# A four-layer graph network on one core: block sums by register-addressed copies, stores in two pieces, scatters over 128 partitions

## The chip, the cores and the metric

The kernel runs on one core of one Trainium2 chip. The metric is the device time of one launch in microseconds (us). Before the change it is 10303.23 us, the median of three runs (10301.11 to 10311.45).

## The reference, cut to what matters

A graph of N = 12500 nodes with 64 features and E = 212500 edges, sorted by `dst`, goes through four layers, each on the normalised output of the one before:

```
for layer in (softmax aggregation, mean aggregation, hyperbolic attention, relational attention):
    h = maximum(layernorm(x), 0)
    x = x + layer(h, src, dst, ...)

# layer 2 (hyperbolic), cut to its end: hh, g are node tables made from h
ex          = exp(e - e_max[row])                      # one number for each edge
denom       = segment_sum(ex, row)                     # row = src, one sum for each node
att_log_h   = segment_sum(ex/denom[row] * log_h[col], row)
z           = elu(att_log_h) ... norm, tanh            # h_prime, added to x

# layer 3 (relational): 8 relations, 4 heads of 16
feat_all    = einsum('ni,rhid->rnhd', h, conv_weights) # per node: 8 x 64 features
el_all, er_all = feat_all . attn_l, feat_all . attn_r  # per node: 8 x 4 each
```

The edges of a layer are summed to nodes in one stage, and a "finish" stage turns the sums into the next layer's node tables.

## The kernel before, in words

Each stage is a `Block` in which every engine has its own hand-written program. A Block begins only when all engines have ended the one before, so the slowest engine, or the last DMA that one of them waits for, sets a stage's end. The order inside an engine is the order of the text. The stages are: the preparation of indices, `softmax_edges(0)`, `finish_softmax`, `mean_edges`, `finish_mean`, `hyperbolic_edges`, `finish_hyperbolic`, `softmax_edges(3)` and `finish_relational`. In the profiled execution `finish_mean` runs from 5685 to 6279 us, `hyperbolic_edges` up to 9477 us and `finish_hyperbolic` from there to 9904 us.

Node data lie on NP = 125 partitions with NB = 100 nodes each (node = p*100 + b). The constant `EVEN` is 112.

`hyperbolic_edges` writes running sums of 65 numbers (denominator and 64 message features) to the DRAM table `run_g`. For each of the BLOCKS = 98 blocks of 128 nodes, `final_g` holds the row of `run_g` from which that block's 128 final rows stand one after another.

`finish_hyperbolic` does the following.

- SyncE (SP) issues `load_indices` (eight loads of the edge indices `src3` into `idx_all`, used only in the next stage), then the load of `final_row`, eight loads of weights, `al` and `ar`. After that it stores one row group of `rows_o` to `table3s` for each of the 100 node groups g, into a ring of DEEP = 4 buffers.
- GpSimd (POOL) waits for `final_row`, gathers the sums of node column b from `run_g` into `acc[:, b, :]` in 100 indirect DMAs over 125 partitions (a quarter of them for each of the semaphores `got_acc[0..3]`), and only then scatters, for each group g, `dst_o[:, g]` to the rows `first_row` of `at_first`, once the group is taken (`lin3.taken`).
- VectorE (DVE) prepares the attention columns of `w_all`, and then for each quarter q of the nodes waits for `got_acc[q]`, computes the layer's output and the layernorm into `Hn`, and signals `h_ready`.
- TensorE (PE) transposes and multiplies one group at a time (`lin3.pe`, five matmuls).
- ScalarE (ACT) runs the roots and exponentials for DVE in between, copies the transposed rows (`lin3.act`) and takes the product into `rows_o` and `dst_o` (`take`). Before group 0 its text has `power(1)`, the exponential for quarter 1, which waits for DVE's `ask_exp` of that quarter. So PE's first product waits for the sums of the first 50 columns.

`finish_mean` is the stage in which the table of the hyperbolic layer is built: POOL gathers the last row of each node from the layer's scan (`gather_last`, 100 gathers over 128 partitions) and scatters the sorted runs (112 scatters). DVE waits for the first 20 gathers before its first product. The table is stored in two halves over 125 partitions at the end.

Of the kernel before, what the change touches and what calls it, by code (L numbers as in the profile page):

```python
# [75 lines left out]
def build(nc, x, src, dst, edge_attr, edge_type, w0a, b0a, gamma, beta, w0b, b0b, scale0,  # L76
          w1, b1, w2, c2, w3, al3, ar3, b3, out):
    with ExitStack() as whole:
# [10 lines left out]
        run_g = dram("run_g", ((NT + 1) * P, ACC2), F32)  # L89
        dst_i = dram("dst_i", (EP,), F32)  # L90
# [37 lines left out]
        first_row = sb("first_row", [NP, NB], I32)  # L128
# [255 lines left out]
        with nc.cleanup_on_exit(), ExitStack() as ctx:  # L384
# [19 lines left out]
            with nc.Block() as block:  # L404
# [37 lines left out]
                def _(dve):  # L442
# [3 lines left out]
                    dve.wait_ge(named, 1)  # L446
# [31 lines left out]
                    step(v.tensor_scalar(first_row[:, :], far_row[:, :], float(HALVES), None, ALU.mult))  # L478
# [1277 lines left out]
        def finish_mean():  # L1756

            with nc.cleanup_on_exit(), ExitStack() as ctx:
# [16 lines left out]
                        "n1_root n1_ask_tanh n1_tanhed n1_ask_log n1_logged n1_p n1_put n1_tabled n1_cready n1_croot n1_scattered", ctx)  # L1775
                nf, s1, tmp, th, np_, s2, k1, tn = (s[:, j, :] for j in range(4, 12))
# [163 lines left out]
        def finish_hyperbolic():  # L1940

            with nc.cleanup_on_exit(), ExitStack() as ctx:
                acc = sb("acc_s", [NP, NB, ACC2], F32, ctx)
                final_row = sb("final_row", [NP, NB], I32, ctx)
# [6 lines left out]
                dst_o = sb("dst_o", [NP, NB, RELS, HEADS], F32, ctx)  # L1951
                lin3 = Linear(ctx, "lin3", D, RELS * ROW3)
                got_acc = counter("n2_got_acc0 n2_got_acc1 n2_got_acc2 n2_got_acc3", ctx)
                got_w, ran, var_ready, std_ready, ask_root, root, ask_tanh, tanhed, ask_exp, exped, h_ready, got_final = counter(
                    "n2_got_w n2_ran n2_var_ready n2_std_ready n2_ask_root n2_root n2_ask_tanh n2_tanhed "
                    "n2_ask_exp n2_exped n2_h n2_got_final", ctx)
                put = counter("n2_put0 n2_put1 n2_put2 n2_put3", ctx)
                put_v, copied, got_idx = counter("n2_putv n2_copied n2_got_idx", ctx)
                EACH = NB // QUARTERS
                den, fac, tmp, zn, th, nf = (s[:, j, :] for j in range(4, 10))  # L1960
                with nc.Block() as block:
                    @block.sync
                    def _(sp):
                        load_indices(sp, src3, got_idx)
# [4 lines left out]
                        for t, a in ((al, al3), (ar, ar3)):  # L1969
                            sp.dma_start(t[:, :], spread_row(a.rearrange("r h d -> (r h d)"), D)).then_inc(got_w, 16)  # L1970
# [178 lines left out]
```

## Time and profile before

| | |
|---|---|
| timed runs | 10303.23 us median, 10301.11 to 10311.45 |
| profiled execution | span 12579.5 us; no other time is given for it, so its span stands for its own time |
| mean granted TensorE clock | 0.618 |
| busy share | PE 53%, DVE 56%, ACT 33%, POOL 59% |
| `finish_mean` | 5685 to 6279 us |
| `finish_hyperbolic` | 9477 to 9904 us |
| DMA queues | POOL's (software) 13.9% of 16 engines, SP's 11.4%, ACT's 8.9% |

The span of the profiled execution is 22% above the timed median. Times in rows are those of the profiled execution, from the start of its span. A row of a timeline has the start, the length, the engine, the line, the operation with its tiles, the count, and in brackets how long the engine was idle before it and what ended that.

### The profile page before, as it was taken

Reading aid. Unit: us, or ns where it says so; the run is one execution under the profiler, and the core shown is the slowest. Engines: PE = TensorE matmul, PEld = TensorE weight load, DVE = VectorE, ACT = ScalarE, POOL = GpSimd, SP = SyncE. Lnnn points to the kernel's source line nnn. Section 1 sums busy time; section 2 is a strip of 40 time slices with the busy share of each in tenths; the row PEclk is TensorE's granted clock in tenths of the full one; section 3 lists DMA queues with packets and bytes.
Section 4 is the critical chain, followed back from the end, with each engine's and each line's share of the span. In section 5 each row is a group of like instructions: output and inputs, shape, how many; then the busy total and the mean of one; then the engine's idle time right before and its main releaser. Section 6 shows DMA issues by size and latency. Waiting matters only on the chain. (4 is left out here: it accounts for less than half of the span.)

```text
span 12579.5 us, 120455 instructions
## 1 busy us (share of the span) xinstructions
PE 6684.8 (53%) x28159; PEld 5276.5 (42%) x28159; DVE 6985.0 (56%) x14192; ACT 4159.8 (33%) x8428; POOL 7375.6 (59%) x7574
## 2 busy tenths in 40 slices
PE   0555555543155555551356666666664655555552
PEld 0333333332145555550356666666662333333331
DVE  4555555565355555531645555555553377777775
ACT  0222222221055555550144444444442222222221
POOL 5666666652666666656055555555556566666665
PEclk9666666665577777775555555555555566666665
DMA  4333333332422222220033333333333344444442
GB/s 88 109 109 109 109 110 111 109 95 25 138 54 56 55 56 55 56 54 16 27 74 78 78 78 77 78 77 78 78 77 66 99 114 112 113 111 114 112 113 80
DMA packets 1318596, 1053.03 MB, mean 84 GB/s; under 512 B 817606, under 2 KB 1034525, under 8 KB 1317680
## 3 DMA queue, kind: packets, MB, share of 16 engines
q0 software_dynamic: 243008, 318.86, 13.9%
q1 hardware_dynamic: 677774, 367.08, 11.4%
q10 hardware_dynamic: 397397, 362.35, 8.9%
q8 instruction: 161, 2.64, 0.1%
q14 instruction: 256, 2.09, 0.1%
HBM read 577.78 MB, written 469.43 MB: 83 GB/s over the span
## 5 line engine op out<-in xcount | busy, mean ns | idle before, releaser
L1172 POOL DMA_INDIRECT h_rows_d<-table,h_idx_d x1840 | 1757.5, 955 | 1405.8 <-PE h_ps_sum L1193 831.4
L640 POOL DMA_INDIRECT rows<-table,idx_all x1664 | 1644.8, 988 | 879.3 <-issue 476.0
L947 POOL DMA_INDIRECT m_rows<-table,idx_all x1664 | 1574.9, 946 | 903.7 <-issue 452.1
L640 POOL DMA_INDIRECT rows<-table3s,idx_all x1664 | 1574.8, 946 | 893.0 <-issue 475.9
L977 PE MATMUL m_ps_sort<-m_hot_high,m_hot_low 128*128 128x224 f32 x3328 | 1050.7, 495 | 972.1 <-issue 817.5
L977 PEld LDWEIGHTS m_ps_sort<-m_hot_high,m_hot_low 128*128 128x128 f32 x3328 | 916.1, 281 | 1077.8 <-issue 938.9
L787 PE MATMUL ps_out<-ident,sums 128*128 128x128 f32 x3328 | 769.6, 397 | 986.9 <-issue 471.4
L1193 PE MATMUL h_ps_sum<-h_rows_d,h_hot 128*128 128x65 f32 x3680 | 829.3, 416 | 659.5 <-DVE h_rows_d L1330 364.9
L787 PEld LDWEIGHTS ps_out<-ident,sums 128*128 128x128 f32 x3328 | 630.3, 220 | 1149.2 <-issue 1041.8
L1193 PEld LDWEIGHTS h_ps_sum<-h_rows_d,h_hot 128*128 128x128 f32 x3680 | 792.7, 327 | 744.0 <-issue 744.0
L1211 PE MATMUL h_ps_src<-h_near,h_hot_t 128*128 128x65 f32 x3680 | 838.1, 419 | 457.9 <-DMA h_near<-table 266.9
L1211 PEld LDWEIGHTS h_ps_src<-h_near,h_hot_t 128*128 128x128 f32 x3680 | 803.2, 331 | 489.7 <-issue 489.0
L1040 DVE TENSOR_TENSOR_SCAN m_sums<-m_same_b,m_sums,m_ps_rows 128x512 f32<-128x512 bf16 x208 | 266.1, 1279 | 1075.2 <-issue 888.9
L827 ACT ACTIVATE out_e<-ps_out 128x512 f32<-128x512 f32 x832 | 445.8, 589 | 1119.2 <-remote 896.6
L1235 ACT ACTIVATE h_hot_t<-h_ps_hot 128x1024 f32<-128x1024 f32 x230 | 235.5, 1024 | 1580.4 <-DMA m_state_b<-scan 1487.7
L658 DVE TENSOR_TENSOR hot<-bins,cat 128x784 bf16<-128x784 bf16 x208 | 202.8, 975 | 945.3 <-DMA rows_p<-dst_i,row_i 848.7
L755 PE MATMUL ps_score<-ident,rows 128*128 128x128 f32 x1664 | 549.7, 425 | 282.4 <-issue 231.8
L1015 ACT ACTIVATE m_hot_low<-m_hot_low,record,m_slope 128x128 f32<-128x128 f32 x1664 | 660.1, 480 | 6.1
L1339 DVE SCALAR_TENSOR_TENSOR h_run<-h_run,h_goes_on,h_ps_sum 128x65 f32<-128x65 f32 x1840 | 518.9, 282 | 248.4 <-DMA final_g<-final_i 14.4
L1079 DVE SCALAR_TENSOR_TENSOR m_junk<-cat,m_ps_base 128x98 f32<-128x98 f32 (+61 forms) x1664 | 593.6, 419 | 91.1 <-issue 51.3
L667 DVE TENSOR_TENSOR_SCAN spread_v<-marks,spread_v,ps_v 64x512 f32<-64x512 bf16 x208 | 263.5, 1267 | 658.3 <-issue 640.0
L813 ACT ACTIVATE score_c<-ps_score 128x512 f32<-128x512 f32 x208 | 124.2, 597 | 1504.6 <-DMA table<-Hn 1219.9
(424 smaller groups left out, 14537.1 us busy)
## 6 DMA issues: line engine op xcount, KB each, us to landing
scan<-out_e ACTq DMA_DIRECT2D x832, 256.0 KB
h_near<-table SPq DMA_DIRECT2D x1840, 32.5 KB
run_g<-h_run ACTq DMA_DIRECT2D x230, 260.0 KB
part_b<-part SPq DMA_DIRECT2D x832, 64.0 KB
max_b<-top ACTq DMA_DIRECT2D x416, 128.0 KB
scan<-m_out_e SPq DMA_DIRECT2D x416, 128.0 KB
attr<-in_edge_attr SPq DMA_DIRECT2D x415, 128.0 KB
h_rows_d<-table,h_idx_d POOLq DMA_INDIRECT x1840
```

Source lines behind the costliest of these rows:

```text
L640: pool.indirect_dma_start(out=rows[:, b, k, h * GW:(h + 1) * GW], out_offset=None, in_=table3s.rearrange("n (q f) -> (n q) f", f=HEADS) if ...
L755: nc.tensor.matmul(ps_score[:, b % 2, k::TILES], rows[:, b, k, :], ident[:, :], start=True, stop=False)
L787: mm = nc.tensor.transpose(ps_out[:, j, k * P:(k + 1) * P], sums[:, b % 2, j, k::TILES], ident[:, :])
L827: ins = a.activation(out_e[:, b, :, :, j * D:(j + 1) * D], ps_out[:, j, :].rearrange("p (k h f) -> p h k f", k=TILES, h=HALVES), ACT.Copy)
L947: pool.indirect_dma_start(out=rows[:, b, k, h * D:(h + 1) * D], out_offset=None, in_=table1, in_offset=bass.IndirectOffsetOnAxis(ap=idx_al ...
L977: nc.tensor.matmul(ps_sort[:, 0:SORTED], hot_low[:, w % 2, j, :], hot_high[:, w % 2, j, :], start=n == 0, stop=n == PC - 1).then_inc(place ...
L1015: ins = a.activation(hot_low[:, w % 2, j, :], hot_low[:, w % 2, j, :], ACT.Relu, bias=record[:, at:at + 1], scale=slope[:, at:at + 1])
L1079: v.scalar_tensor_tensor(junk[:, at % 4, 0:BLOCKS + n], cat[:, p, 0:BLOCKS + n], cat[:, p, BLOCKS + n:BLOCKS + n + 1], ps_base[:, 0:BLOCKS ...
L1172: pool.indirect_dma_start(out=rows_d[:, b, k, :], out_offset=None, in_=table2, in_offset=bass.IndirectOffsetOnAxis(ap=idx_d[:, c * BT + k: ...
L1193: mm = nc.tensor.matmul(ps_sum[:, k // HB, (k % HB) * ACC2:(k % HB + 1) * ACC2], hot[:, b, k, :], rows_d[:, b, k, D + 1:ROW2], start=True, ...
L1211: mm = nc.tensor.matmul(ps_src[:, k // HB, (k % HB) * (D + 1):(k % HB + 1) * (D + 1)], hot_t[:, b % 2, k * P:(k + 1) * P], near[:, b, k, : ...
L1339: v.scalar_tensor_tensor(run[:, b, k, :], before, goes_on[:, bass.ds(c * BT + k, 1)], ps_sum[:, k // HB, (k % HB) * ACC2:(k % HB + 1) * AC ...
```

## The change

Four things change.

1. **Block sums.** A new DRAM tensor `acc_g` holds the final sums in node order. `finish_mean` loads the 98 first rows into `final_s` on one partition. In `finish_hyperbolic` SP and ACT each read 49 of these numbers into registers, seven at a time, and issue 49 copies from DRAM to DRAM of 128 rows each. When all 98 have landed, SP loads `acc` from `acc_g`, each quarter in two pieces. The 100 gathers and `final_row` are gone, so POOL has nothing before its scatters but a memset.
2. **Indices earlier.** `load_indices` for the last layer moves from `finish_hyperbolic` to SP's list in `finish_mean`.
3. **Stores in two pieces.** The two stores of the hyperbolic table in `finish_mean` and the 100 stores to `table3s` are split into partitions 0 to 111 and 112 to 124.
4. **Scatters over 128 partitions.** `first_row` and `dst_o` get 128 partitions; the three added ones scatter zeros to rows that nothing reads.

```diff
+        acc_g = dram("acc_g", (BLOCKS * P, ACC2), F32)
-        first_row = sb("first_row", [NP, NB], I32)
+        first_row = sb("first_row", [P, NB], I32)
+        final_s = sb("final_s", [1, BLOCKS], I32)
...
@@ preparation, POOL @@
+                    pool.iota(first_row[:, :], pattern=[[2, NB]], base=EP - 2 * N, channel_multiplier=2 * NB).then_inc(named, 1)
...
@@ finish_mean, SP @@
+                        sp.dma_start(final_s[:, :], final_g.rearrange("(b n) -> n b", n=P)[0:1, :],
+                                     allow_slow_non_contiguous=True).then_inc(got_final, 16)
+                        load_indices(sp, src3, got_idx)
                         for h, at in enumerate(halves):
                             sp.wait_ge(tabled, h + 1)
-                            sp.dma_start(nodes(table2[0:N, :])[:, at, :], table[:, at, :]).then_inc(put, 16)
-                        sp.wait_ge(put, 32)
+                            for some in (slice(0, EVEN), slice(EVEN, NP)):
+                                sp.dma_start(nodes(table2[0:N, :])[some, at, :], table[some, at, :]).then_inc(put, 16)
+                        sp.wait_ge(put, 64)
...
@@ finish_hyperbolic @@
+                FETCH = 7
+                def fetch_sums(eng, kind, lo, hi):
+                    for b0 in range(lo, hi, FETCH):
+                        _, rows = nc.values_load_multi_w_load_instructions(
+                            final_s[0:1, b0:b0 + FETCH], engines=(kind,), min_val=0, max_val=NT * P)
+                        for j, at in enumerate(rows):
+                            eng.dma_start(acc_g[(b0 + j) * P:(b0 + j + 1) * P, :], run_g[bass.ds(at, P), :]).then_inc(fetched, 16)
@@ finish_hyperbolic, SP @@
-                        load_indices(sp, src3, got_idx)
-                        sp.dma_start(final_row[:, :], final_g[0:N].rearrange("(p b) -> p b", p=NP)).then_inc(got_final, 16)
+                        fetch_sums(sp, mybir.EngineType.SP, 0, BLOCKS // 2)
 ...
+                        sp.wait_ge(fetched, 16 * BLOCKS)
+                        for q in range(QUARTERS):
+                            for some in (slice(0, EVEN), slice(EVEN, NP)):
+                                sp.dma_start(acc[some, quarter(q), :], nodes(acc_g[0:N, :])[some, quarter(q), :]).then_inc(got_acc[q], 16)
                         for g in range(NB):
                             sp.wait_ge(copied, g + 1)
-                            sp.dma_start(t3s[:, g, :], rows_o[:, g % DEEP, :, :].rearrange("p r f -> p (r f)")).then_inc(put[g % DEEP], 16)
+                            for some in (slice(0, EVEN), slice(EVEN, NP)):
+                                sp.dma_start(t3s[some, g, :], rows_o[some, g % DEEP, :, :].rearrange("p r f -> p (r f)")).then_inc(put[g % DEEP], 16)
@@ finish_hyperbolic, POOL @@
-                        pool.wait_ge(got_final, 16)
-                        for b in range(NB):
-                            pool.indirect_dma_start(out=acc[:, b, :], out_offset=None, in_=run_g,
-                                                    in_offset=bass.IndirectOffsetOnAxis(ap=final_row[:, b:b + 1], axis=0)).then_inc(got_acc[b * QUARTERS // NB], 16)
+                        pool.memset(dst_o[NP - NP % 32:P, :, :, :], 0.0).then_inc(blank, 1)
@@ finish_hyperbolic, ACT @@
+                        fetch_sums(act, mybir.EngineType.Activation, BLOCKS // 2, BLOCKS)
                         for part in chain:
                             part(0)
+                        act.wait_ge(blank, 1)
@@ finish_hyperbolic, DVE @@
-                            dve.wait_ge(got_acc[q], 16 * NB // QUARTERS)
+                            dve.wait_ge(got_acc[q], 32)
```

On SP in `finish_mean` the list stood like this before the change (`w_s` is the tile of `w2`, `table` the hyperbolic node table in DRAM):

```order
L1782 DMA w_rows<-in_L_gnn_W 64x128
L1783 DMA w_s<-in_L_gnn_W 64x64
L1784 DMA b_row<-in_L_gnn_b 125x64
L1785 DMA c_cols<-in_L_gnn_c 128x1
L1788 DMA table<-table_s 125x6500 x2
L1779 UNCONDITIONAL_BRANCH
```

After the change SP's list in the same stage reads:

```order
L1789 DMA c_cols<-in_L_gnn_c 128x1
L1790 DMA final_s<-final_g 1x98x1
L171 DMA idx_all<-src 128x52x4 x8
L1796 DMA table<-table_s 112x6500
L1796 DMA table<-table_s 13x6500
L1796 DMA table<-table_s 112x6500
L1796 DMA table<-table_s 13x6500
```

Nine DMAs have come in ahead of the two table stores, and each store has become two.

On SP at the start of `finish_hyperbolic` the whole list before the change was:

```order
L169 DMA idx_all<-src 128x52x4 x8
L1965 DMA final_row<-final_g 125x100
L1967 DMA w_all<-in_L_gnn_conv_weights 64x4x16 x8
L1970 DMA al<-in_L_gnn_attn_l 64x512
L1970 DMA ar<-in_L_gnn_attn_r 64x512
L1974 DMA table3s<-rows_o 125x576 x100
```

After the change SP begins with seven turns of one register read, 14 register instructions (ISA) and seven pairs of an address move and a copy; the start of the first turn is:

```order
L1975 TENSOR_LOAD final_s
L1975 ISA x14
L1978 ISA
L1978 DMA acc_g<-run_g 16x520
L1978 ISA
L1978 DMA acc_g<-run_g 16x520
L1978 ISA
L1978 DMA acc_g<-run_g 16x520
```

Behind the seventh turn follow the loads of weights and then those of `acc`:

```order
L1978 DMA acc_g<-run_g 16x520
L1984 DMA w_all<-in_L_gnn_conv_weights 64x4x16 x8
L1987 DMA al<-in_L_gnn_attn_l 64x512
L1987 DMA ar<-in_L_gnn_attn_r 64x512
L1991 DMA acc_s<-acc_g 112x1625
L1991 DMA acc_s<-acc_g 13x1625
```

The weights now stand behind 49 copies instead of behind nine loads, and ACT's list has the same seven turns ahead of its first activation.

## Rows read from the trace of the kernel before

**Rows 1.** The page's first line.

```profile
span 12579.5 us, 120455 instructions
```

**Rows 2.** Waits of `finish_hyperbolic`: engine, line, waited for, total us, times, longest us.

```profile
PE lin_ps_y L1409 <- ACT lin_rows_t L1422: 46.3, 14, 20.2
ACT rows_o L2022 <- DMA table3s<-rows_o: 74.9, 34, 5.5
```

**Rows 3.** Timeline of SP, start of `finish_hyperbolic`.

```profile
9476.66 3.51 SPq L169 DMA_DIRECT2D idx_all<-src  x2
...
9508.05 5.31 SPq L1967 DMA_DIRECT2D w_all<-in_L_gnn_conv_weights  x8
...
9514.06 0.60 SPq L1970 DMA_DIRECT2D ar<-in_L_gnn_attn_r  x1
```

**Rows 4.** Timeline of DVE in `finish_hyperbolic`, quarters 0 and 1.

```profile
9517.63 0.68 DVE L2047 TENSOR_TENSOR wa<-w_all,al 64x512 f32<-64x512 f32 x1 [46.26 <-DMA ar<-in_L_gnn_attn_r]
...
9520.49 0.68 DVE L2049 TENSOR_REDUCE w_all<-wa 64x32 f32<-64x512 f32 x1
9549.70 0.19 DVE L2055 TENSOR_SCALAR s2s<-acc_s 125x25 f32<-125x25 f32 x1 [28.53 <-DMA acc_s<-run_g,final_row]
...
9578.54 0.99 DVE L202 TENSOR_SCALAR Hn<-Hn 125x1600 f32<-125x1600 f32 x1
9595.23 0.18 DVE L2055 TENSOR_SCALAR s2s<-acc_s 125x25 f32<-125x25 f32 x1 [15.70 <-DMA acc_s<-run_g,final_row]
```

**Rows 5.** Timeline of PE, its first product and one at quarter 2's start.

```profile
9600.49 2.39 PE L1409 MATMUL lin_ps_y<-w_all,lin_rows_t 64*125 64x304 f32 x4 [20.22 <-ACT lin_rows_t L1422]
...
9759.71 2.39 PE L1409 MATMUL lin_ps_y<-w_all,lin_rows_t 64*125 64x304 f32 x4 [4.94 <-ACT lin_rows_t L1422]
```

**Rows 6.** Timeline of ACT (first and last take) and of the stage's end.

```profile
9602.91 0.65 ACT L2022 ACTIVATE rows_o<-lin_ps_y 125x576 f32<-125x576 f32 x1 [2.32 <-PE lin_ps_y L1409]
...
9892.20 0.65 ACT L2022 ACTIVATE rows_o<-lin_ps_y 125x576 f32<-125x576 f32 x1 [1.29 <-PE lin_ps_y L1409]
...
9904.04 0.06 DVE L650 MEMSET top<- 128x1 f32 x1 [93.67 <-PEq L1942]
```

**Rows 7.** Timeline of SP, the first register-addressed copies of `hyperbolic_edges`.

```profile
6290.89 8.81 SPq L1157 DMA_DIRECT2D h_near<-table  x11
```

**Rows 8.** The same copies by tile: ns min/median/max, first and last start.

```profile
L1157 SPq DMA_DIRECT2D h_near<-table x4: 332/333/333, 6292.0 to 6293.6; - x4
L1157 SPq MOVE h_near<-table x3: 29/29/29, 6292.5 to 6293.5; - x3
...
L1157 SPq MOVE h_near<-table x3: 3/693/711, 6301.5 to 6303.7; - x3
```

**Rows 9.** Timeline of SP, the second half-table's store and the next stage.

```profile
6252.65 0.28 SPq L1788 DMA_DIRECT2D table<-table_s  x1
6279.45 0.22 SPq L1141 DMA_DIRECT2D h_block_s<-block_g  x1
```

**Rows 10.** Windows: us, engines' busy, clock, DMA share of 16 engines, GB/s.

```profile
6253.00:6278.00 25.00, 0.00 (x0) 0.00 (x0) 0.00 (x0) 0.00 (x0) 0.00 (x0) 0.50 0.31 130
11.00:20.00 9.00, 0.00 (x0) 0.00 (x0) 0.00 (x0) 0.00 (x0) 0.00 (x0) 1.00 0.98 296
```

**Rows 11.** Timeline of POOL: long gathers beside the first index load.

```profile
69.38 7.40 POOL L435 DMA_INDIRECT rows_p<-dst_i,row_i  x1 [0.30 <-issue]
77.08 6.56 POOL L435 DMA_INDIRECT rows_p<-dst_i,row_i  x1 [0.30 <-issue]
...
92.70 10.10 POOL L435 DMA_INDIRECT rows_p<-dst_i,row_i  x1 [0.30 <-issue]
```

**Rows 12.** Timeline of POOL, start of `finish_mean`.

```profile
5692.10 7.09 POOL L1356 DMA_INDIRECT table_s<-scan,last_edge  x1 [0.30 <-issue]
5699.50 0.94 POOL L1356 DMA_INDIRECT table_s<-scan,last_edge  x1 [0.30 <-issue]
```

**Rows 13.** Timeline of DVE, its first wait for a gather in `finish_mean`.

```profile
5718.31 1.49 DVE L1873 TENSOR_TENSOR G<-table_s,s 125x1280 f32<-125x1280 f32 x1 [19.24 <-DMA table_s<-scan,last_edge]
```

More of the change, by code:

```diff
@@ L445, in _ @@
                     step(v.memset(zero1[:, :], 0.0))
-                    dve.wait_ge(named, 1)
+                    dve.wait_ge(named, 2)
                     step(v.memset(ones_c[:, :], 1.0))
@@ L1943, in finish_hyperbolic @@
                 acc = sb("acc_s", [NP, NB, ACC2], F32, ctx)
-                final_row = sb("final_row", [NP, NB], I32, ctx)
                 w_all = sb("w3_all", [D, RELS, ROW3], F32, ctx)
@@ L1950, in finish_hyperbolic @@
                 rows_o = sb("rows_o", [NP, DEEP, RELS, SRC3], F32, ctx)
-                dst_o = sb("dst_o", [NP, NB, RELS, HEADS], F32, ctx)
+                dst_o = sb("dst_o", [P, NB, RELS, HEADS], F32, ctx)
                 lin3 = Linear(ctx, "lin3", D, RELS * ROW3)
                 got_acc = counter("n2_got_acc0 n2_got_acc1 n2_got_acc2 n2_got_acc3", ctx)
-                got_w, ran, var_ready, std_ready, ask_root, root, ask_tanh, tanhed, ask_exp, exped, h_ready, got_final = counter(
+                got_w, ran, var_ready, std_ready, ask_root, root, ask_tanh, tanhed, ask_exp, exped, h_ready, fetched, blank = counter(
                     "n2_got_w n2_ran n2_var_ready n2_std_ready n2_ask_root n2_root n2_ask_tanh n2_tanhed "
-                    "n2_ask_exp n2_exped n2_h n2_got_final", ctx)
+                    "n2_ask_exp n2_exped n2_h n2_fetched n2_blank", ctx)
                 put = counter("n2_put0 n2_put1 n2_put2 n2_put3", ctx)
-                put_v, copied, got_idx = counter("n2_putv n2_copied n2_got_idx", ctx)
+                put_v, copied = counter("n2_putv n2_copied", ctx)
+                FETCH = 7
                 EACH = NB // QUARTERS
                 den, fac, tmp, zn, th, nf = (s[:, j, :] for j in range(4, 10))
+                def fetch_sums(eng, kind, lo, hi):
[4 more added lines that the diff above has]
+                            eng.dma_start(acc_g[(b0 + j) * P:(b0 + j + 1) * P, :], run_g[bass.ds(at, P), :]).then_inc(fetched, 16)
                 with nc.Block() as block:
@@ L1973, in _ @@
                             sp.wait_ge(copied, g + 1)
[L1974 removed]
+                            for some in (slice(0, EVEN), slice(EVEN, NP)):
+                                sp.dma_start(t3s[some, g, :], rows_o[some, g % DEEP, :, :].rearrange("p r f -> p (r f)")).then_inc(put[g % DEEP], 16)
                         for b in range(DEEP):
[L1976 to L1977 removed]
+                            sp.wait_ge(put[b], 32 * NB // DEEP)
                     @block.gpsimd
                     def _(pool):
[L1981 to L1984 removed]
+                        pool.memset(dst_o[NP - NP % 32:P, :, :, :], 0.0).then_inc(blank, 1)
                         for g in range(NB):
@@ L2019, in take @@
                             if g >= DEEP:
-                                act.wait_ge(put[g % DEEP], 16 * (g // DEEP))
+                                act.wait_ge(put[g % DEEP], 32 * (g // DEEP))
                             both = lin3.ps_y[:, g % 2, :, 0:RELS * ROW3 // 2].rearrange("p t (r f) -> p t r f", f=ROW3)
@@ L2023, in take @@
                                          ACT.Copy).then_inc(copied, 1)
-                            a.activation(dst_o[:, g, :, :].rearrange("p (t r) f -> p t r f", t=2), both[:, :, :, SRC3:ROW3],
+                            a.activation(dst_o[0:NP, g, :, :].rearrange("p (t r) f -> p t r f", t=2), both[:, :, :, SRC3:ROW3],
                                          ACT.Copy).then_inc(lin3.taken, 1)
                         chain = (power, length, bend, deviation)
+                        fetch_sums(act, mybir.EngineType.Activation, BLOCKS // 2, BLOCKS)
                         for part in chain:
                             part(0)
+                        act.wait_ge(blank, 1)
                         for q in range(QUARTERS):
```

7 lines of the change are left out of this document (4 added, 3 removed).

## The prediction

> **What bounds the kernel now.** I first looked for the stages that the change touches, since a stage ends with its slowest engine and stages do not overlap. The span is 12579.5 us [rows 1], and the changed lines lie in about 1000 us of it, in two finish stages. The big edge stages keep their text. So only what ends last in `finish_mean` and `finish_hyperbolic` counts.
>
> In `finish_hyperbolic` I read the waits, and then the timelines of the engines. Four pieces follow each other there.
>
> - SP starts at 9476.7 with the index loads and reaches the weights only at 9508.1 and `ar` at 9514.1 [rows 3]. POOL's gathers start about then, behind `final_row`, which stands behind the index loads.
> - DVE prepares the weights from 9517.6 to 9521.2, then waits 28.5 us for the first quarter of the gathers, to 9549.7. It ends quarter 0 at 9579.5 and waits 15.7 us for quarter 1's gathers, to 9595.2 [rows 4]. ACT's `power(1)` stands ahead of group 0, so PE's first product comes only at 9600.5 [rows 5], 5.3 us behind DVE's start on quarter 1.
> - From the first take at 9602.9 to the last at 9892.2 there are 99 groups in 289.3 us [rows 6]. PE was idle 46.3 us for ACT's transposed rows, of which 20.2 us is the wait before the first product; so 26.1 us of idle lie in the stream [rows 2]. The rest is (289.3 - 26.1)/99 = 2.66 us a group, which is PE's own pace. ACT in turn waited 74.9 us, 34 times, for `table3s` stores to free the ring [rows 2].
> - 11.8 us from the last take to the next stage [rows 6].
>
> So PE's stream is the bound, with a late start, and with stalls that come from the store ring.
>
> In `finish_mean` two waits are touched. DVE waits 19.2 us for the first 20 gathers, until 5718.3 [rows 13]. At the end all engines wait for the second half-table's store, from 6252.9 to 6279.45, 26.5 us [rows 9].
>
> **The change part by part.**
>
> *Preparation.* One more small index pattern on POOL ahead of 100 gathers. It is too small to weigh: 0.
>
> *Index loads in `finish_mean`.* On SP itself the nine added DMAs are hidden: its next work is 500 us later. But they run beside POOL's gathers. The same eight loads do so already in the preparation, and there three of the first 25 gathers took 7.40, 6.56 and 10.10 us [rows 11], where a plain one takes 0.94 [rows 12], which is 6.46 + 5.62 + 9.16 = 21.2 us lost. Without such loads, in `finish_mean` today, one gather of the first 20 takes 7.09, a loss of 6.1 us [rows 12]. The difference is 15 us, it falls before the 20th gather, and DVE is waiting for exactly that one [rows 13]. So +15 us; bounds 0 (the loads slip in between) and +31 (all the 31.4 us that SP took for them and `final_row` in `finish_hyperbolic`, from 9476.7 to 9508.1 [rows 3]).
>
> *Stores of the table in two pieces.* The half-table is 125 x 50 x 130 numbers of 4 bytes, 3.25 MB, and moved at 130 GB/s with a DMA share of 0.31 [rows 10]. That is 25.0 of the 26.5 us. 0.31 is 5/16: a 125-partition transfer kept 5 of the 16 engines busy. The input `X` is loaded in the very pieces the change uses, 112 and 13 partitions, and there the share is 0.98 at 296 GB/s [rows 10]. At this rate 3.25 MB takes 11.0 us, 14 less; for the second piece I leave 1 and take -13. Bounds 0, and -17 if the rate followed the share (130/0.31 = 419 GB/s, 7.8 us). The first half's store lies beside DVE's work and gives nothing.
>
> The Trainium skill, DMA: Bandwidth & Descriptors, "Rules for kernel authors", speaks against this edit: two transfers to disjoint partition halves serialize and are not worth it. The same page, "Why a DMA increments its semaphore by 16 and not by 1", says that the engine count is the largest number up to 16 that divides the slowest dimension, which is 5 for 125 and 16 for 112. By the first rule this term would be 0 or a little above, by the second it stands; the trace's 0.31 agrees with the second.
>
> *The front of `finish_hyperbolic`.* SP now starts with 49 copies. Register-addressed copies of the same size exist: 11 of them were issued in 8.81 us with one register read of eight numbers among them [rows 7], and four in a row started 0.53 us apart (6292.0 to 6293.6) [rows 8]. So a read costs 8.81 - 11 x 0.53 = 3.0 us, and seven turns cost 49 x 0.53 + 7 x 3.0 = 47 us. ACT does its 49 alongside; it has nothing else then. The data, 3.3 MB, needs 11 us at 296 GB/s and is hidden in that. Weights: `w_all` to the end of `ar` took 6.6 us of issue and landed 3.0 us later [rows 3, 4]: 9476.7 + 47 + 6.6 + 3.0 = 9533.3, and DVE's preparation of 3.6 us ends at 9536.9. The first two loads of `acc` (0.8 MB, 3 us, and the 3 us to land) come at about the same time. So DVE starts quarter 0 at 9537 in place of 9549.7: -13. It ends 29.8 us later, at 9566.7; quarter 1's sums are there, so PE's first product comes 5.3 us after, at 9572 in place of 9600.5: -28 together. The index loads and `final_row` that left SP are in this count, since the start is now the 9476.7 of rows 3. Bounds of the term: at no pause for the reads 26 us in place of 47, so -49; the other end is the first rival.
>
> *The stream.* POOL had its gathers to finish first, then caught up with back-to-back scatters, and ACT waited for stores that five engines carried beside them. Now each scatter follows its take at once, and each store of 0.29 MB has 16 engines. The store waits go. What stays of PE's 26.1 us: at the starts of quarters 1 and 2 ACT loads a table and does an exponential between groups, which I put at 10 us together (the stall at quarter 2's start was 4.9 us long [rows 5]). So -16; bounds -26 and 0. 128 in place of 125 partitions costs POOL nothing that is waited for, since it has 2.66 us for each scatter. SP's second store for each group also fits in 2.66, if it is issued like the copies of rows 8 (0.33). The memset of `dst_o` on idle POOL is hidden behind ACT's copies.
>
> *Tail.* 11.8 us, unchanged: 0.
>
> Sum in the profiled execution: +15 - 13 - 28 - 16 = -42 us. The timed median is 10303.23/12579.5 = 0.82 of the span. The trace does not say which pieces are shorter in a timed run: DMA and PE terms may keep their size, the instruction terms may shrink. Between -42 and 0.82 x -42 = -34 I take the middle, -38: 10265 us.
>
> **The rivals.**
>
> *Slow issue (ends slower).* Later in that same list single register moves on SP took 0.69 to 0.71 us in place of 0.03 [rows 8]. If SP runs its seven turns at 0.70 us an instruction, 7 x 29 = 203 instructions cost 142 us in place of 47, +95, and DVE and PE start that much later: -42 + 95 = +53, by 0.91 (38/42, as above) +48, 10351 us. It decides from the point where the seven turns take 47 + 42 = 89 us. For it: new straight-line text on SP and ACT, which had no such list here. Against it: the slow moves came when POOL had begun its gathers, while POOL is idle during the copies.
>
> *The index loads hit harder and the stores gain little.* +31 in place of +15 and, with the pieces running one behind the other, 0 in place of -13: -42 + 16 + 13 = -13, by 0.91 -12: 10291 us, no change that can be told. For it: on the end of `finish_mean` nothing but the store is running, so any cost of the second piece shows. Against it: the share of 0.98 in the same pieces [rows 10]. The page's rule on disjoint halves leads to this side.
>
> *The stream does not gain.* If ACT's waits for stores have another cause than the five engines and POOL's catching up, say the sixteen-engine scatters that now meet each store, the -16 goes: -26, by 0.91 -24: 10279 us. For it: the scatters' short rows. Against it: the waits stopped once POOL had caught up.
>
> *More than forecast.* The index loads cost nothing in `finish_mean`: -57, by 0.91 -52: 10251 us. For it: they start a few gathers later than in the preparation.
>
> **How the numbers follow.** A difference under about 0.2%, 21 us, cannot be told from none. Forecast 0.45 (own range 10255 to 10278), more than forecast 0.15, the stream does not gain 0.12, index loads and stores 0.14, slow issue 0.14. Faster: the first two and most of the third, 0.45 + 0.15 + 0.10 = 0.70. Same: the rest of the third, the fourth and a part of slow issue at a milder pace, 0.02 + 0.13 + 0.02 = 0.17. Slower 0.13. The range reaches to 10240 on the low side (the front at its bound of -49 brings -21 more with part of the rest), and to 10310 on the high side, which leaves out most of the slow issue and little else.
>
> **What would show it.** In the profile after: the second half-table's store should hold up the stage 12 to 15 us, with a DMA share near 1; DVE's first product in `finish_mean` should come some 15 us later, with two or three gathers of 6 to 10 us beside the index loads; SP's copies should take 40 to 55 us; DVE should not wait between quarters 0 and 1; ACT's waits for `table3s` should fall from 74.9 us to a few. The prediction is wrong if SP's seven turns take over 89 us, if DVE's first start in `finish_hyperbolic` is later than 73 us into the stage, or if PE's idle inside the stream stays above 20 us.

## The result, and the profile after

| | median us | range | runs |
|---|---|---|---|
| before | 10302.17 | 10294.27 to 10311.45 | 4 |
| after | 10248.46 | 10246.65 to 10251.74 | 4 |

The ratio is 0.9949, 95% interval 0.9938 to 0.996: 54 us less. The forecast was 10265, range 10240 to 10310.

One thing must be said before any row is compared. The profile of before had a span of 12579.5 us [rows 1], and the level at which a program runs differs from one set of runs to the next: of the three sets below, two ran the kernel before at 12522.6 and 12342.1 us (the higher level) and one at 10299.95 (the lower level). So I compare single stages, and kernels of one set.

The page after begins so.

```profile
span 10250.0 us, 120975 instructions
```

Its waits in `finish_hyperbolic` (engine, line, waited for, total us, times, longest us), against [rows 2]:

```profile
POOL at_first L2005 <- ACT dst_o L2042: 266.8, 100, 107.4
ACT rows_o L2040 <- PE lin_ps_y L1412: 163.2, 97, 2.3
...
DVE wa L2067 <- DMA ar<-in_L_gnn_attn_r: 70.9, 1, 70.9
...
PE lin_ps_y L1412 <- ACT lin_rows_t L1425: 13.0, 4, 6.0
...
DVE s2s L2075 <- DMA acc_s<-acc_g: 1.3, 1, 1.3
```

The row "ACT rows_o <- DMA table3s" (74.9 us) is gone, ACT waits for PE at 97 of the 100 takes, and PE's waits for ACT fell from 46.3 to 13.0. Of these 13.0, 6.0 stand before PE's first product, so PE's idle inside the stream fell from 26.1 to 7.0 us, where the forecast left 10.

The timeline of SP at the start of the stage, against [rows 3], and of DVE, against [rows 4]:

```profile
7523.95 53.49 SPq L1978 DMA_DIRECT2D acc_g<-run_g  x49
7577.48 5.34 SPq L1984 DMA_DIRECT2D w_all<-in_L_gnn_conv_weights  x8
7582.87 0.61 SPq L1987 DMA_DIRECT2D al<-in_L_gnn_attn_l  x1
7583.52 0.61 SPq L1987 DMA_DIRECT2D ar<-in_L_gnn_attn_r  x1
7584.17 3.98 SPq L1991 DMA_DIRECT2D acc_s<-acc_g  x8
```

```profile
7586.80 0.68 DVE L2067 TENSOR_TENSOR wa<-w_all,al 64x512 f32<-64x512 f32 x1 [70.95 <-DMA ar<-in_L_gnn_attn_r]
...
7591.64 0.18 DVE L2075 TENSOR_SCALAR s2s<-acc_s 125x25 f32<-125x25 f32 x1 [1.31 <-DMA acc_s<-acc_g]
...
7621.14 0.18 DVE L2075 TENSOR_SCALAR s2s<-acc_s 125x25 f32<-125x25 f32 x1
```

The stage starts with SP's first register read, at 7521.0 (by tile):

```profile
L1975 SPq TENSOR_LOAD <-final_s x7: 940/1467/1484, 7521.0 to 7569.5; - x7
```

DVE starts quarter 0 after 70.6 us (73.0 before), and quarter 1 at once behind it, where it had waited 15.7 us.

First and last take on ACT, and the next stage, against [rows 6]:

```profile
7630.16 0.65 ACT L2040 ACTIVATE rows_o<-lin_ps_y 125x576 f32<-125x576 f32 x1 [2.32 <-PE lin_ps_y L1412]
...
7899.11 0.65 ACT L2040 ACTIVATE rows_o<-lin_ps_y 125x576 f32<-125x576 f32 x1 [1.29 <-PE lin_ps_y L1412]
```

The 99 groups between them take 268.9 us, where they took 289.3.

The end of `finish_mean`, on SP, against [rows 9], and its window, against [rows 10]:

```profile
5101.14 45.71 SPq L1796 DMA_DIRECT2D table<-table_s  x4
5159.97 0.23 SPq L1144 DMA_DIRECT2D h_block_s<-block_g  x1
```

```profile
5147.00:5160.00 13.00, 0.00 (x0) 0.00 (x0) 0.00 (x0) 0.00 (x0) 0.01 (x1) 0.50 0.69 226
```

The last stores are issued at 5146.85, and the next stage starts 13.1 us later, at 226 GB/s and a DMA share of 0.69, in place of 26.5 us at 130 and 0.31. The time is what the forecast said (12 to 15 us); the share is not "near 1", and the rate is below the 296 GB/s that it was worked out from.

### The profile page after: what moved, and what is told of

The parts are those of the page before. It is cut to its first block and busy times, and to the rows that moved or that the text cites. A ratio compares the mean times of both kernels' runs of the same rounds, so it can differ in the third digit from the quotient of the medians.

```text
span 10250.0 us, 120975 instructions
## 1 busy us (share of the span) xinstructions
PE 6757.6 (66%) x28159; PEld 5282.8 (52%) x28159; DVE 6974.8 (68%) x14192; ACT 4156.6 (41%) x8428; POOL 7329.3 (72%) x7476
## 5 line engine op out<-in xcount | busy, mean ns | idle before, releaser
L643 POOL DMA_INDIRECT rows<-table3s,idx_all x1664 | 1626.8, 978 | 518.3 <-issue 507.1
L980 PE MATMUL m_ps_sort<-m_hot_high,m_hot_low 128*128 128x224 f32 x3328 | 931.5, 452 | 620.2 <-DVE m_hot_high L1074 540.4
L980 PEld LDWEIGHTS m_ps_sort<-m_hot_high,m_hot_low 128*128 128x128 f32 x3328 | 818.7, 251 | 704.2 <-DVE m_hot_high L1074 573.5
L758 PE MATMUL ps_score<-ident,rows 128*128 128x128 f32 x1664 | 634.0, 483 | 599.4 <-DMA rows<-table,idx_all 595.1
L790 PE MATMUL ps_out<-ident,sums 128*128 128x128 f32 x3328 | 723.2, 388 | 283.2 <-DVE sums L713 283.2
L758 PEld LDWEIGHTS ps_score<-ident,rows 128*128 128x128 f32 x1664 | 402.2, 301 | 851.9 <-issue 851.9
L818 ACT ACTIVATE ps_score<-ps_score 128x512 f32<-128x512 f32 x208 | 121.1, 582 | 1608.6 <-PE ps_score L760 1608.6
L807 ACT ACTIVATE wide<-rows 128x256 f32<-128x256 f32 x416 | 149.9, 407 | 1489.4 <-DMA rows<-table3s,idx_all 1489.4
L760 PE MATMUL ps_score<-ident,attr 128*64 128x128 f32 x3328 | 564.2, 438 | 0.0
```

What stands on the lines that cost most here:

```text
L643: pool.indirect_dma_start(out=rows[:, b, k, h * GW:(h + 1) * GW], out_offset=None, in_=table3s.rearrange("n (q f) -> (n q) f", f=HEADS) if ...
L758: nc.tensor.matmul(ps_score[:, b % 2, k::TILES], rows[:, b, k, :], ident[:, :], start=True, stop=False)
L760: mm = nc.tensor.matmul(ps_score[h * D:(h + 1) * D, b % 2, k::TILES], attr[:, b, h, k, :], ident[:, :], start=False, stop=True)
L790: mm = nc.tensor.transpose(ps_out[:, j, k * P:(k + 1) * P], sums[:, b % 2, j, k::TILES], ident[:, :])
L980: nc.tensor.matmul(ps_sort[:, 0:SORTED], hot_low[:, w % 2, j, :], hot_high[:, w % 2, j, :], start=n == 0, stop=n == PC - 1).then_inc(place ...
```

## The experiments

For each kernel I read the same four lengths: `finish_mean`, and in `finish_hyperbolic` the front (stage start to first take), the takes (first to last) and the tail (last take to SP's first load of the next stage). "x" marks a set at the higher level, in which `finish_mean` is some 215 us longer, and only comparable with others marked x.

| kernel | `finish_mean` | front | takes | tail |
|---|---|---|---|---|
| before_again | 594.0 x | 126.0 | 292.7 | 12.1 |
| b_pieces_only | 363.7 | 126.1 | 268.9 | 7.4 |
| b_scatter_128 | 376.6 | 127.7 | 273.5 | 15.9 |
| after_again | 363.8 | 108.5 | 268.9 | 13.5 |
| a_rows_whole | 579.0 x | 108.3 | 268.9 | 16.4 |
| a_rows_whole_scatter_125 | 363.9 | 108.5 | 280.4 | 12.8 |
| a_table_whole | 592.0 x | 108.0 | 268.9 | 13.4 |
| a_idx_back | 580.4 x | 137.2 | 269.1 | 13.4 |
| a_scatter_125 | 578.6 x | 108.8 | 268.9 | 7.4 |
| a_fetch_14 | 578.7 x | 105.7 | 269.1 | 13.5 |
| a_three_queues | 578.7 x | 86.6 | 268.9 | 15.8 |
| a_best | 572.3 x | 85.9 | 268.9 | 7.8 |

### The levels: before and after once more

`before_again` is the kernel before, unchanged.

> The kernel before, once more, for its profile. Its first profile had a span of 12579.5 us beside timed runs of 10303. Theory (that one profiled execution was disturbed, in stretches of straight-line code beside POOL's gathers): the span now lies within 20 us of 10303, single register moves on SP take about 0.03 us there, finish_mean takes about 375 us in place of 594, and the stages not touched agree with the profile after. Rival (this kernel is always slow there when it is profiled, or the old text provokes it): span over 12000 us again, and SP's moves at 0.7 us.

One run, 12529.1 us, beside 15 timed runs of the same kernel of 12506.8 to 12536.4. The first theory fell: it was not one disturbed execution. Its rival falls too: `b_pieces_only`, with the old text outside of its stores, was profiled at 10255.7 us in the next set. The SP moves of the copies in `hyperbolic_edges` (by tile: ns min/median/max) read

```profile
L1157 SPq MOVE h_near<-table x1840: 2/29/1422, 6273.6 to 9411.7; - x184
```

and in `b_pieces_only`, which has the same text there and ran at the lower level,

```profile
L1157 SPq MOVE h_near<-table x1840: 29/29/37, 5165.5 to 7456.1; - x184
```

The median is the same; only some moves are long. The level lies in the edge stages, in `finish_softmax` (366.9 us here, 282.9 in `b_pieces_only`) and in `finish_mean`. In `finish_mean` DVE sat idle 204.9 us ahead of eight of its 25 takes of PE's products in the trace of before, which the profile puts down to a DMA of the stage ahead, and 31.2 us ahead of 17 of them in `b_scatter_128`, put down to PE. That is most of the difference between the levels there; since that DMA had long ended, what DVE really waited for is open. `finish_hyperbolic` does not follow the level: front, takes and tail add up to 390.9 us in `after_again` and to 390.3 in `a_table_whole`, which ran at the higher one, against 430.8 here.

> The changed kernel once more, to stand beside the others of this set and beside the kernel before on one chip. The first set ran the kernel before at 12522.6 us in place of 10302, with the edge stages longer and finish_hyperbolic as it was, so the level belongs to the chip or the day and not to one profile. Theory (what the change removes is transfers and waits of the two finish stages, which keep their size at either level): 52 to 56 us under the kernel before, whatever its level; finish_hyperbolic 389 us against 431, finish_mean 13 to 15 us shorter. Rival (the gain depends on the level): a difference under 40 or over 70 us.

`after_again` is the changed kernel. 10247.6 us (10241.9 to 10251.9) beside 10299.95 for before: ratio 0.9951 (0.9937 to 0.9964), 52 us. As expected, and within the first result. This set at 10299.95 us and the one at 12522.6 carry the same chip number on record (2), the one at 12342.1 another (8), so the chip alone does not explain the level.

### The table's store

`a_table_whole`:

```diff
-for some in (slice(0, EVEN), slice(EVEN, NP)):
-    sp.dma_start(nodes(table2[0:N, :])[some, at, :], table[some, at, :])
+sp.dma_start(nodes(table2[0:N, :])[:, at, :], table[:, at, :])
```

> The changed kernel, with finish_mean's table stores in one piece of 125 partitions. Theory (five engines carry a 125-partition store, sixteen and one the pieces): the last store takes some 25 us in place of 12.6, DMA share 0.31, +13 us, 10261 us. Rival (two pieces on disjoint partitions run one behind the other, and the shorter wait seen after has another cause): 10248 us.

Timed 0.9964 (0.995 to 0.9978) of before, and the changed kernel was not in this set. The stage decides: `finish_mean` 592.0 us, against 580.4 and 579.0 in the two kernels of the set that had the pieces: +12 to +13. The same at the lower level: 376.6 whole (`b_scatter_128`), 363.7 in pieces (`b_pieces_only`). The windows of these two, from the last stores to the next stage, have share and GB/s

```profile
5144.00:5169.00 25.00, 0.00 (x0) 0.00 (x0) 0.00 (x0) 0.00 (x0) 0.00 (x0) 0.50 0.29 125
```

```profile
5140.00:5153.00 13.00, 0.00 (x0) 0.00 (x0) 0.00 (x0) 0.00 (x0) 0.00 (x0) 0.50 0.77 250
```

So the pieces together take half the time of the whole store: 13.1 us in place of 26.5. The "sixteen and one" engines of the theory are not shown; no trace says how many engines carry the 13 partitions.

### The index loads

`a_idx_back` moves `load_indices(sp, src3, got_idx)` from `finish_mean` back to the head of SP's text in `finish_hyperbolic`, ahead of the copies.

> The changed kernel, with the index loads back at the start of finish_hyperbolic, ahead of SP's copies. In the profile after they take SP 30.4 us, and DVE's first product in finish_mean came only 2.4 us later than before. Theory (the front of finish_hyperbolic is SP's list, and the loads cost finish_mean next to nothing): +30 in front, -2 in finish_mean, 10276 us. Rival 1 (as predicted, they cost 15 us in finish_mean): +30 - 15, 10263 us. Rival 2 (the front is bound by ACT's copies and the sums, not by SP): 10246 us.

Timed 12508.5 us, 0.9989 (0.998 to 0.9998) of before. The front grew from 108.5 to 137.2, +29, and `finish_mean` did not get shorter: 580.4 against 579.0. The theory holds in the stages. (The two timed medians are 14 us apart, where the stages would leave some 25; the interval, 2.5 to 25 us, does not decide.) `b_pieces_only` shows why my 15 us were wrong. It has no index loads in `finish_mean`, and POOL's sixth gather there reads

```profile
4796.86 6.72 POOL L1356 DMA_INDIRECT table_s<-scan,last_edge  x1 [0.30 <-issue]
```

while `after_again`, with the loads beside it, has

```profile
4793.31 6.72 POOL L1359 DMA_INDIRECT table_s<-scan,last_edge  x1 [0.30 <-issue]
```

It is the same gather and the same length, and all others around it take 0.94 to 1.0 in both. So the long gather of `finish_mean` is not made by the index loads. What makes it is open, and so is what makes the three of [rows 11]: no kernel here leaves the loads out of the preparation. With the loads DVE's first product stood 35.4 us into the stage, without them 32.8, and that did not reach the stage's end: 363.8 against 363.7.

### Stores, scatters, and who waited for the ring

The forecast said that the ring's stores waited because of five engines and POOL's catching up, both at once. Four kernels separate them.

`a_rows_whole`, the changed kernel with

```diff
-for some in (slice(0, EVEN), slice(EVEN, NP)):
-    sp.dma_start(t3s[some, g, :], rows_o[some, g % DEEP, :, :]...)
+sp.dma_start(t3s[:, g, :], rows_o[:, g % DEEP, :, :]...)
```

(and the waits on `put` halved):

> The changed kernel, with the stores of table3s in finish_hyperbolic in one piece of 125 partitions. Theory (the five-engine stores freed the ring too late, ACT waited and PE with it): ACT waits for table3s again, about 60 us in all, PE's idle for ACT rises by some 16 us, 10264 us. Rival (the waits came from POOL catching up with scatters behind its 100 gathers, which no longer happens): ACT's waits stay under 10 us, 10248 us.

0.996 (0.9946 to 0.9974) of before; takes 268.9, no wait for `table3s`, tail 16.4 in place of 13.5. My theory failed here: with 128-partition scatters the pieces of these stores are worth 3 us. Hence two new ones, S and C.

`a_rows_whole_scatter_125` also has

```diff
-ap=first_row[:, g:g + 1] ... in_=dst_o[:, g, :, :]
+ap=first_row[0:NP, g:g + 1] ... in_=dst_o[0:NP, g, :, :]
```

> The changed kernel, with the table3s stores whole and the scatters over 125 partitions, as both were before; the copies stay. With the stores alone whole the 100 takes of finish_hyperbolic still ran through in 268.9 us without a wait for table3s, only the tail grew by 3. Theory S (in the kernel before five-engine stores and five-engine scatters shared the same engines, and either edit alone is enough): the takes spread to some 280 to 290 us and ACT waits for table3s 50 to 100 us; about +17 to +20 in this stage. Theory C (the waits came only while POOL caught up behind its 100 gathers, which the copies removed): takes 269 us, tail 3 us longer, no waits for table3s.

Takes 280.4, 11.5 us more than in `after_again`, where the theory had 17 to 20 for the stage. Timed 10251.6 us, 0.9951 (0.9938 to 0.9965), only 4 us above `after_again`; its five runs went from 10246.2 to 10259.1, and the profiled one is the longest of them, so the timed runs do not show all of the 11.5. And the wait is back without any gathers ahead of the scatters:

```profile
ACT rows_o L2039 <- DMA table3s<-rows_o: 71.3, 35, 4.1
```

`b_scatter_128` is the kernel before with `first_row` and `dst_o` on 128 partitions (and the blank rows of both set), `b_pieces_only` the kernel before with the stores of both stages in two pieces.

> The kernel before, with the scatters of finish_hyperbolic over 128 partitions and nothing else. It had 289 to 293 us from the first to the last take, and 75 to 109 us of ACT's waits for table3s. Theory S (shared five engines): the waits for table3s go and the takes need about 270 us, -20 us. Theory C (POOL's catching up floods the queues): little changes, within 5 us.

> The kernel before, with the stores of both stages in two pieces and nothing else. finish_mean should be 13 us shorter in any case. Theory S (five-engine stores and scatters share their engines): with sixteen engines for the stores ACT's waits for table3s go, the takes need about 270 us, -20 in finish_hyperbolic and -3 at its tail, some -36 in all. Theory C (POOL's catching up): the waits stay, takes about 285 to 293 us, some -16 in all.

`b_scatter_128`: 10289.3 us, 0.999 (0.9981 to 0.9999), takes 273.5, the wait for `table3s` down from 108.6 to

```profile
ACT rows_o L2024 <- DMA table3s<-rows_o: 22.2, 10, 2.9
```

`b_pieces_only`: 10257.7 us, 0.996 (0.9946 to 0.9974), 42 us under before. Takes 268.9, no wait left, and ACT is bound by PE just as in the changed kernel:

```profile
ACT rows_o L2024 <- PE lin_ps_y L1409: 163.2, 97, 2.3
```

Theory S holds for the most part: 125-partition stores and 125-partition scatters are slow only together. The pieces alone take all waits away, the 128-partition scatters alone leave 22.2 us of them and 4.6 us in the takes.

C has a share, larger than the totals say, for POOL's lag decides where the time is lost. In the trace of before the scatter of group 0 started 75.6 us behind its take and that of group 50 only 3.5 us behind. Up to the take of group 50 the kernel needed 159.2 us and from there 130.1; `b_pieces_only` needed 139.0 and 129.9. So all 20 us were lost while POOL caught up, and 31 of the 34 waits fell there. In `before_again` it was 156.3 and 136.4: most of the loss, not all. In `a_rows_whole_scatter_125`, where POOL has no gathers to catch up for, it is 139.8 and 140.6: the same stores and scatters still lose 11 us, but only late in the stream. With stores and scatters as they were, the copies in place of the gathers bring the takes from 292.7 (289.3 in the first trace) to 280.4, and in the 128-partition pair from 273.5 to 268.9.

The windows of 50 us in the stream show what the core's DMA engines do, first `a_rows_whole_scatter_125`, then `after_again` (busy PE, PEld, DVE, ACT, POOL, clock, share, GB/s):

```profile
7758.00:7808.00 50.00, 44.33 (x85) 21.56 (x84) 19.48 (x19) 20.11 (x55) 21.62 (x16) 0.50 0.42 101
```

```profile
7752.00:7802.00 50.00, 47.15 (x89) 22.88 (x89) 19.48 (x19) 22.28 (x60) 20.44 (x18) 0.50 0.36 108
```

More data at a smaller share. That five engines were the shared ones is inferred from these and the 0.31 of [rows 10]; the trace does not name the engine of a packet.

### The scatters at the tail

`a_scatter_125`: the changed kernel with the second diff above alone.

> The changed kernel with its scatters over 125 partitions again; copies and stores in pieces stay. The kernel before with the pieces alone had all 100 takes in 268.9 us and 7.4 us from the last take to the next stage, the changed kernel 268.9 and 13.5. Theory (once the stores are in pieces the 128-partition scatters give nothing and cost 6 us at the tail): takes 269 us, tail 7.5 us, 6 us under the changed kernel, a ratio of 0.9945 to the kernel before. Rival (the shorter tail there came from POOL being late and not from the scatters): tail 13 us, no difference.

12275.0 us, 0.9943 (0.993 to 0.9956). Takes 268.9, tail 7.4 in place of 13.5. The timelines of POOL at the end of the stage, the last scatter and the first gather of the next stage, in `after_again`

```profile
7888.22 0.97 POOL L2005 DMA_INDIRECT at_first<-dst_o,first_row  x1 [1.06 <-ACT dst_o L2042]
...
7900.47 0.98 POOL L643 DMA_INDIRECT rows<-table3s,idx_all  x1 [11.28 <-POOLq L1952]
```

and in `a_scatter_125`

```profile
9672.70 1.18 POOL L2005 DMA_INDIRECT at_first<-dst_o,first_row  x1 [0.85 <-ACT dst_o L2042]
...
9678.90 0.98 POOL L643 DMA_INDIRECT rows<-table3s,idx_all  x1 [5.02 <-POOLq L1952]
```

The 128-partition scatter occupies POOL 0.2 us less, and the next stage starts 6 us later. So in the changed kernel the scatters' edit is a loss of 6 us, once the stores are in pieces. The data are not late. POOL passed its last wait 2.3 us after the last scatter's start in `after_again` and 2.7 us in `a_scatter_125`. What follows is a DRAIN, an instruction at the end of the Block that the timeline leaves out. By source line it reads, in `after_again`

```profile
L1979 POOLq DRAIN  x1: 8217/8217/8217, 7890.7 to 7890.7; - x1
```

and in `a_scatter_125`

```profile
L1979 POOLq DRAIN  x1: 1847/1847/1847, 9675.5 to 9675.5; - x1
```

It lasts 1.85 to 1.87 us in all six traces with 125-partition scatters and 8.22 us in seven of the eight with 128 (10.52 in `a_three_queues`), whatever the stores and the copies. Its 6.4 us are the difference. What POOL does in it no trace says.

### The front

`a_fetch_14` sets `FETCH = 14`, so 4 register reads in place of 7.

> The changed kernel with fourteen block offsets read at a time in place of seven: 4 reads on each of SP and ACT in place of 7. A turn of seven copies took SP 8.1 us, of which seven copies at 0.52 and their moves are 3.7, the arithmetic and asserts for seven values 1.2, and some 3.3 us belong to the read itself. Theory (the front of finish_hyperbolic is the sum of these instructions): 3 x 3.3 = 10 us off, SP's copies in 46 to 47 us, DVE's first quarter at some 60 us into the stage, 0.9941 of the kernel before. Rival (the copies' data or ACT's list ends last): the first quarter stays at 70, no difference.

Its timed runs went from 12114 to 12302 us and the ratio, 0.9881 (0.9831 to 0.993), is set by two of the six runs, at 12114 and 12118 us, 160 us under the other four, so the level moves within a set too. It says nothing of a few us; the trace does: front 105.7 in place of 108.5, a gain of 3 and not of 10. The rows of `after_again` say why. The reads by line (SP alone; ns min/median/max):

```profile
L1975 SPq FUSED_REGOPS  x49: 147/147/155, 7510.8 to 7561.3; - x49
L1975 SPq SEQ_ASSERT  x49: 18/18/24, 7511.0 to 7561.5; - x49
...
L1975 SPq TENSOR_LOAD <-final_s x7: 942/1465/1482, 7509.8 to 7558.3; - x7
```

and the copies, by tile and in a window inside one turn:

```profile
L1978 SPq DMA_DIRECT2D acc_g<-run_g x49: 492/492/644, 7512.8 to 7565.7; - x49
```

```profile
7516.06 1.17 SPq L1978 DMA_DIRECT2D acc_g<-run_g  x2
```

A read costs 1.5 us. The rest of a turn goes with the values: 0.24 us of arithmetic and assert each (1.7 for seven), and copies 0.68 apart (4.8 for seven), 8.0 together. Three reads fewer are 4.4 at most, and the four reads of fourteen took 1.2, 2.9, 1.2 and 1.5. The expectation had put 3.3 us on a read, which in truth is a read with the arithmetic of its seven values, and that arithmetic does not get less.

`a_three_queues`: the weight loads moved to POOL, SP's waits fitted to the new counts, and

```diff
-fetch_sums(sp, mybir.EngineType.SP, 0, BLOCKS // 2)
+fetch_sums(sp, mybir.EngineType.SP, 28, 63, fetched)
-fetch_sums(act, mybir.EngineType.Activation, BLOCKS // 2, BLOCKS)
+fetch_sums(act, mybir.EngineType.Activation, 63, BLOCKS, fetched)
+fetch_sums(pool, mybir.EngineType.Pool, 0, 28, fetched_p)
```

> The changed kernel with the 98 copies on three engines (SP 35, ACT 35, POOL 28) and the ten weight loads on POOL in place of SP. Theory (SP's and ACT's lists set the front): five turns in place of seven, -16, and the weight loads off SP, -6.6: DVE's first quarter some 22 us earlier, 0.9930 of the kernel before. Rival (POOL, which takes about 1 us for each of its DMAs, becomes the last: 38 DMAs and four reads, 50 us and more): first quarter at some 60 to 70 us, gain under 10.

Front 86.6 in place of 108.5: -22, as the theory had it. The rival fails in its price: seven direct copies took POOL 3.4 to 3.9 us, not 7. DVE has its weights early and waits for the sums alone:

```profile
9292.75 0.68 DVE L2069 TENSOR_TENSOR wa<-w_all,al 64x512 f32<-64x512 f32 x1 [14.63 <-DMA ar<-in_L_gnn_attn_r]
...
9331.33 0.18 DVE L2077 TENSOR_SCALAR s2s<-acc_s 125x25 f32<-125x25 f32 x1 [35.04 <-DMA acc_s<-acc_g]
```

The tail is 2.3 us longer, with POOL's DRAIN at 10.52 us in place of 8.22. Timed it is 0.9946 (0.9933 to 0.9959), which does not separate it from the changed kernel (0.9951 in its own set; it was not in this one).

`a_best` joins these: three queues, `FETCH = 14`, 125-partition scatters, and three more stores in pieces, of `table0`, `table1` and `out`.

> All that the runs point to in one kernel: copies on three engines with fourteen offsets a read, scatters over 125 partitions, and the stores of the first table, of the second table and of the output in two pieces as well. By the terms: -22 (three queues), -6 (fewer reads), -6 (scatters), and 0.64 MB at 130 against 296 GB/s, -2.7 us, at the end of finish_softmax and of finish_relational each: 39 us under the changed kernel, 10208 us where that is at 10248, 0.9913 of the kernel before. Rival (the front is then bound by POOL's list or by ACT's): 15 to 20 us under it.

12264.8 us, 0.9936 (0.9917 to 0.9955) of before, where 0.9913 was expected. By stages beside `a_scatter_125` of the same set: `finish_softmax` 363.4 for 366.8, `finish_mean` 572.3 for 578.6 (not expected, and not explained), `finish_relational` 155.6 for 158.8, and `finish_hyperbolic` 28 us under the changed kernel. But two edge stages of unchanged text differ by more between these traces (`hyperbolic_edges` 3090.5 and 3079.1 us, the last `softmax_edges` 2506.1 and 2454.5), so in total time it is not shown to beat the changed kernel.

## Why the prediction was right, and which of its terms were not

The sign, the stages and the waits that go were right; two terms were mis-sized by 10 and 15 us, one by 4 to 8, and one, the tail, was left out. The errors of index loads and front point opposite ways, so that the total came within 17 us of the result is in part luck. Lengths in us:

| term | forecast | measured | from |
|---|---|---|---|
| index loads in `finish_mean` | +15 | 0 | 363.8 against 363.7 |
| table store in pieces | -13 | -13 | 363.7 against 376.6 |
| front | -28 | -18 | 108.5 against 126.1 |
| stream | -16 | -20 to -24 | 268.9 against 289.3 and 292.7 |
| tail | 0 | +1 | 13.5 against 12.1 to 12.7 |
| sum | -42, scaled to -38 | -50 to -54 | timed -52 and -54 |

- *Index loads.* The step that failed is the reading of [rows 11] as loads hindering gathers. In `finish_mean` the one long gather stands at the same place with and without them; DVE's first product came 2.4 us later than before, not 15. My rival "more than forecast" (10251) had just this case and came nearest.
- *Table store.* Right in size: 13.1 us in place of 26.5. Of the mechanism the runs show that the pieces are faster together at twice the share; the share itself was 0.69 to 0.77, not near 1, and the number of engines is inferred from it. The Trainium skill (DMA: Bandwidth & Descriptors, "Rules for kernel authors") says that transfers to disjoint partition halves serialize, and advises one transfer of 128 partitions instead. These runs do not show that for 112 + 13 partitions against one of 125; the measurement decides.
- *Front.* Seven turns took 56.5 us (7521.0 to 7577.5), not 47. The term was mis-sized in the spacing of the copies, 0.68 in place of the 0.53 of [rows 8] (the issue of one took 0.49 and not 0.33), 49 x 0.15 = 7 us, and in the read with its arithmetic, 3.3 in place of 3.0, 2 us. DVE's start came at 70.6 and not at 60, and no wait followed between the quarters, as forecast.
- *Stream.* The waits for the ring went. That the stores' engines matter was right; that POOL's catching up is needed for the waits was not, since they come back without it (`a_rows_whole_scatter_125`), though in the kernel before nearly all of the loss fell in it. The forecast left out the scatters' own 125 partitions: with them at 128 the waits shrink to 22.2 us without the pieces.
- *Tail.* Forecast at 0; in truth -5 from the pieces and +6 from the 128-partition scatters, a cost that I had not seen because I priced the scatter by POOL's time for each and not by the DRAIN that closes the stage (8.22 against 1.85 us).
- *Scaling.* The factor 0.91 had no ground. The touched lengths are equal at both levels; what differs between 12500 and 10300 is in the edge stages, in `finish_softmax` and in other parts of `finish_mean`. Unscaled and with the index loads at 0, the sum is -57.
- *Slow issue.* It did not come: SP's 49 copies took 53.5 us at the lower level and 53.5 at the higher (`a_scatter_125`).

Put alone on the kernel before, the stores in pieces give four fifths of the gain (42 of 52 us in one set); copies, moved loads and scatters together add 10. The shares depend on the order. Taken out of the changed kernel the pieces are worth 13 us (table) and 3 us (rows), because the copies and the 128-partition scatters had by then removed most of what the row pieces remove.

## What to carry to other kernels

- Where a store from 125 partitions stands at a stage's end or feeds a ring beside other 125-partition transfers, split it into 112 + 13 first: one line, and here alone four fifths of the whole gain. The sign to look for was a DMA share of 0.31 beside an otherwise idle core.
- Price an edit at a stage's end by when the next stage starts, not by the time that the engine spends on each transfer: look at every instruction between the last transfer and the next stage, those that the timeline leaves out too.
- Where two edits may remove the same wait, run each alone on the kernel before and leave each out of the kernel after: the two differences are not the same.
- Before two losses of engine time are blamed on each other because they stand side by side, look for the same loss where the suspect is absent.

## What the runs showed of the hardware

- The same program ran at 10300, 12342 and 12522 us in three sets, always at a mean clock of 0.62. At the two higher levels the stages that stretched were the edge stages, `finish_softmax` and `finish_mean`, while the preparation, `finish_hyperbolic` and `finish_relational` kept their lengths (in the changed kernel 234, 391 and 158.7 us). The cause is open.
- A register-addressed copy of a 128-row block cost SP 0.68 us, and its offset 0.24 us of arithmetic and assert, at seven and at fourteen values a read; the read itself took 0.9 to 1.5 us for seven and 1.2 to 2.9 for fourteen.
- An indirect scatter over 128 partitions of 32 numbers each occupied POOL 0.97 us against 1.18 over 125. The DRAIN on POOL at the end of the stage took 8.22 us after such scatters over 128 partitions and 1.85 over 125.
- A store of 3.25 MB from 125 partitions took 26.5 us at a DMA share of 0.29 to 0.31; as 112 and 13 partitions it took 13.1 us at 0.69 to 0.77.
